# One transformer layer on one core: the next head's loads in sixteen pieces, the softmax division moved to Pool's queue, an output phase with four buffers

## The reference

```python
xn = layernorm(x)                                 # x: 2 x 4096 tokens x 256
q, k, v = (xn @ W.T + b for each of Wq, Wk, Wv)   # 16 heads of 16 channels, q scaled
probs = softmax(einsum('bqhd,bkhd->bhqk', q, k))  # 4096 x 4096 for each of 2 x 16 heads
out = einsum('bhqk,bkhd->bqhd', probs, v)
attn = out @ Wo.T + bo
x = x + attn + routed_ffn(xn)                     # 8 experts, weights from a router
```

## Time and profile before

| | before |
|---|---|
| median of 3 runs | 7455.96 us (7396.34 to 7465.76) |
| the profiled execution | 7403.4 us, its span 7401.6 us |
| PE busy | 6831.7 us, 92% of the span |
| DVE busy | 5743.0 us, 78% |
| ACT busy | 4988.7 us, 67% |
| attention phase | first score about 1511 us, last copy of `pv` at 7058.4 us |
| output phase | 7058.4 to 7401.6 us |

### The profile page before, as it was taken

One profiled execution on the slowest core, in us unless ns is written; L12 is line 12 of the kernel. 1 busy time (PEld: TensorE's weight loads), 2 busy tenths in 40 slices (PEclk: granted clock), 3 DMA queues, 4 the chain that ended last, 5 costly groups with the idle time before them and its releaser, 6 DMA issues. The chain is left out here.

```text
span 7401.6 us, 159847 instructions
## 1 busy us (share of the span) xinstructions
PE 6831.7 (92%) x57168; PEld 3216.6 (43%) x57168; DVE 5743.0 (78%) x6069; ACT 4988.7 (67%) x9109; POOL 423.5 (6%) x367
## 2 busy tenths in 40 slices
PE   7999999699999999999999999999999999999932
PEld 6888888433333333333333333333333333333322
DVE  4544555499989899988898999989889899889611
ACT  3333333168878788877787888878778788778810
POOL 2222322100000000000000000000000000000001
PEclk9999999789989999998898999999889899899965
DMA  2111111111212211111111111122111111111023
GB/s 84 46 46 48 43 41 49 27 21 22 28 21 29 29 22 22 22 22 22 23 22 22 22 22 22 24 31 29 22 22 23 22 22 22 22 22 23 3 88 100
DMA packets 243392, 232.05 MB, mean 31 GB/s; under 512 B 154512, under 2 KB 206992, under 8 KB 236432
## 3 DMA queue, kind: packets, MB, share of 16 engines
q1 hardware_dynamic: 242576, 221.09, 17.9%
HBM read 150.74 MB, written 68.16 MB: 30 GB/s over the span
## 5 line engine op out<-in xcount | busy, mean ns | idle before, releaser
L810 DVE TENSOR_REDUCE mx<-sc 128x1 f32<-128x1024 f32 x4096 | 5007.9, 1224 | 565.8 <-PE sc L699 537.6
L793 ACT ACTIVATE pr<-st 128x512 f32<-128x512 f32 x8192 | 4448.3, 595 | 1046.4 <-PE st L708 763.4
L721 PE MATMUL pv<-pr,vst 128*32 128x256 f32 x32768 | 2761.6, 410 | 14.7 <-ACT oT L780 13.3
L708 PE MATMUL st<-qr,kr 50*128 50x512 f32 x8192 | 2143.9, 518 | 98.8 <-issue 77.4
L699 PE MATMUL sc<-kr,qr 48*128 48x512 f32 x8192 | 1731.4, 417 | 135.2 <-issue 67.9
L708 PEld LDWEIGHTS st<-qr,kr 50*128 50x128 f32 x8192 | 795.3, 190 | 1908.0 <-ACT pr L793 1799.9
L721 PEld LDWEIGHTS pv<-pr,vst 128*32 128x32 f32 x32768 | 661.3, 110 | 1667.1 <-issue 996.1
L699 PEld LDWEIGHTS sc<-kr,qr 48*128 48x128 f32 x8192 | 831.6, 200 | 107.7 <-DVE mx L810 67.3
L393 ACT ACTIVATE gated<-gate 128x512 f32<-128x512 f32 x256 | 152.0, 598 | 637.2 <-PE up L72 637.0
L561 DVE TENSOR_TENSOR hraw<-gated,up 128x512 f32<-128x512 f32 x256 | 173.4, 686 | 431.8 <-ACT gated L393 428.9
L72 PE MATMUL gate<-xT,experts 128*128 128x512 f32 x1536 | 410.5, 404 | 11.3 <-issue 11.3
(11 more groups left out here) (93 smaller groups left out, 1370.2 us busy)
## 6 DMA issues: line engine op xcount, KB each, us to landing
qr<-parts_d SPq DMA_DIRECT2D x192, 256.0 KB, 8.7
kr<-parts_d SPq DMA_DIRECT2D x192, 256.0 KB, 19.5
parts_d<-part SPq DMA_DIRECT2D x64, 512.0 KB, 3.0
x_in<-in_L_attn_hidden_states SPq DMA_DIRECT2D x16, 512.0 KB, 4.5
v_d<-v_sb SPq DMA_DIRECT2D x32, 256.0 KB, 2.1
base_d<-base SPq DMA_DIRECT2D x16, 512.0 KB, 3.2
vst<-v_d SPq DMA_DIRECT2D x32, 256.0 KB, 25.3
sums_d<-oT SPq DMA_DIRECT2D x256, 32.0 KB
```

The source lines that it names most:

```text
L708: nc.tensor.matmul(st[(x + grp) % STB][:, :], kr[par][r0:r0 + ROWSM, kb * P:(kb + 1) * P], qr[par][r0:r0 + ROWSM, q0:q0 + GT], start=True, ...
L721: last = nc.tensor.matmul(pv[VC * j:VC * (j + 1), cols], vst[par][:, kb, :], pr[:, (QSUB * kb + j) % PRING, cols], start=(kb == 0 and half ...
L793: nc.scalar.activation(pr[:, (QSUB * kb + j) % PRING, :], st[x % STB][:, :], ACT.Exp).then_inc(st_read, 1)
L810: nc.vector.reduce_max(mx[par][:, u // MAXU, u % MAXU:u % MAXU + 1], sc[u % 2][:, :], AX.X).then_inc(sc_read, 1)
```

## The change

Attention phase: the twelve loads of q and k are spread over key blocks 1 to 17 of the head's first step, one or two blocks apart, in reversed order, each behind a wait on the count of finished blocks. v is loaded in four parts behind blocks 5, 10, 15 and 20 of the head's second step. The division moves here: for every head Pool's queue loads the 4096 denominators as 128 x 32, DVE inverts them in block 14 of the next head's first step, Pool's queue stores them, loads sums and broadcast reciprocals as 128 x 512 each, POOL multiplies, and the quotients go to a new DRAM tensor `attn_d`. Output phase: two loads for each group instead of nineteen, four buffers instead of two, no loop, results stored from Pool's queue, and PE waits for the sum of group g-2 instead of g-1.

```diff
         QK_LOADS = 2 * 3 * 2
+        V_LOADS = 4
+        QK_EVERY, V_EVERY = 3, 5
...
+            def load(n, par, piece):
+                w, rest = divmod(QK_LOADS - 1 - piece, QK_LOADS // 2)
+                grp, term = divmod(rest, 3)
+                dst, hl = ((qr, (0, 1, 0)), (kr, (0, 0, 1)))[w]
+                r0 = 64 * grp + HD * term
+                sp.dma_start(dst[par][r0:r0 + HD, :].bitcast(F32), c.parts_d[w, hl[term], bass.ds(n * HD, HD), :]).then_inc(qk_loaded, DMA)
+            def load_v(n, par, piece):
+                kbs = KB // V_LOADS
+                sp.dma_start(vst[par][:, piece * kbs:(piece + 1) * kbs, 0:HD],
+                             c.v_d[bass.ds((n // H) * S + piece * kbs * P, kbs * P), bass.ds((n % H) * HD, HD)].rearrange("(t p) d -> p t d", p=P)
+                             ).then_inc(v_loaded, DMA)
...
                     if hf == 0 and not ending:
                         wait_alone(sp, st_full, s * SLOTS + 1, passed)
-                        load(n + 1, 1 - par)
                         wait_alone(sp, pv_done, s * KB + PV_PRE, passed)
-                        load_v(n + 1, 1 - par)
+                        for piece in range(QK_LOADS):
+                            wait_alone(sp, pv_done, s * KB + PV_PRE + 1 + QK_EVERY * piece // 2, passed)
+                            load(n + 1, 1 - par, piece)
                     if not (ending and hf):
                         wait_alone(sp, st_read, s * SLOTS + ROWS_SLOT + 2 + READ_PRE, passed)
                         rows(par if hf == 0 else 1 - par, 1 - hf)
                     sums(s, n, hf)
+                    if hf == 0 and not ending:
+                        for piece in range(V_LOADS):
+                            wait_alone(sp, pv_done, (s + 1) * KB + PV_PRE + V_EVERY * (piece + 1), passed)
+                            load_v(n + 1, 1 - par, piece)
...
+            def divide(n):
+                wait_alone(pool, sums_stored, ((n + 1) * 2 * SUM_STORES + 1) * DMA, passed)
+                nc.gpsimd.dma_start(den[:, :], c.den_d[bass.ds(n, 1), :].rearrange("o (p f) -> (o p) f", p=P)).then_inc(den_in, DMA)
+                wait_alone(pool, den_inverted, n + 1, passed)
+                nc.gpsimd.dma_start(c.rden_d[bass.ds(n, 1), :].rearrange("o (p f) -> (o p) f", p=P), rden[:, :]).then_inc(rden_stored, DMA)
+                nc.gpsimd.dma_start(whole[:, :], c.sums_d[bass.ds(n * HD, HD), :].rearrange("r (x t) -> r x t", t=GT)).then_inc(parts_in, DMA)
+                wait_alone(pool, rden_stored, (n + 1) * DMA, passed)
+                nc.gpsimd.dma_start(recs[:, :], c.rden_d[bass.ds(n, 1), :].rearrange("o (x t) -> o x t", t=GT).broadcast_to([HD, S // GT, GT])).then_inc(parts_in, DMA)
+                wait_alone(pool, parts_in, (n + 1) * 2 * DMA, passed)
+                nc.gpsimd.tensor_tensor(whole[:, :], whole[:, :], recs[:, :], ALU.mult).then_inc(divided, 1)
+                wait_alone(pool, divided, n + 1, passed)
+                nc.gpsimd.dma_start(c.attn_d[bass.ds(n * HD, HD), :].rearrange("r (x t) -> r x t", t=GT), whole[:, :]).then_inc(attn_stored, DMA)
+                wait_alone(pool, attn_stored, (n + 1) * DMA, passed)
+            with pool.Fori(0, HEADS) as n:
+                divide(n)
...
-                                    pe.wait_ge(v_loaded, (n + 1) * DMA)
+                                    pe.wait_ge(v_loaded, (n + 1) * V_LOADS * DMA)
...
+            def inverted(n):
+                dve.wait_ge(den_in, (n + 1) * DMA)
+                if not isinstance(n, int) or n:
+                    dve.wait_ge(rden_stored, n * DMA)
+                nc.vector.reciprocal(rden[:, :], den[:, :]).then_inc(den_inverted, 1)
...
+                        if kb == DIVIDE_AT and q % 2 == 0 and not (first and q == 0):
+                            inverted(RING * i + q // 2 - 1)
 
             rolled(dve, body)
+            inverted(HEADS - 1)
...
+        DEEP = 4
...
+            for g in range(NG):
+                i, b, c0 = g % DEEP, g // GPB, (g % GPB) * GT
+                if g >= DEEP:
+                    sp.wait_ge(low_ready, (g - DEEP + 1) * KC)
+                sp.dma_start(attn[i][:, :, :], c.attn_d[b * D:(b + 1) * D, c0:c0 + GT].rearrange("(k p) t -> p k t", p=P)).then_inc(attn_in[i], DMA)
+                if g >= DEEP:
+                    sp.wait_ge(stored[i], (g // DEEP) * DMA)
+                sp.dma_start(base[i][:, :, :], tokens_of(c.base_d, g)).then_inc(base_in[i], DMA)
+            for i in range(DEEP):
+                sp.wait_ge(stored[i], (NG // DEEP) * DMA)
...
+                pool.wait_ge(sum_ready, g + 1)
+                nc.gpsimd.dma_start(tokens_of(a["out"], g), base[g % DEEP][:, :, :]).then_inc(stored[g % DEEP], DMA)
...
+                pe.wait_ge(low_ready, (g + 1) * KC)
+                if g >= 2:
+                    pe.wait_ge(sum_ready, g - 1)
```

More of the change, by code:

```diff
@@ L878, in output_phase @@
         sum_ready = sem("sum_ready")
-        SUM_LOADS = KC + H
         block = ctx.enter_context(nc.Block())
         def tokens_of(dram, g):
[L883 to L892, removed]
+            return dram[g * GT:(g + 1) * GT, :].rearrange("(t p) d -> p t d", p=P)
@@ L894, in _ @@
         @block.sync
         def _(sp):
[L896 to L916, removed]
@@ L936, in _ @@
-            rolled(pool, body)
+            for g in range(NG):
+                pool.wait_ge(sum_ready, g + 1)
+                nc.gpsimd.dma_start(tokens_of(a["out"], g), base[g % DEEP][:, :, :]).then_inc(stored[g % DEEP], DMA)
         @block.tensor
         def _(pe):
-            def body(g, par, first, last):
-                pe.wait_ge(low_ready, g * KC + KC)
-                pe.wait_ge(sum_ready, g + 1)
+            for g in range(NG):
+                pe.wait_ge(low_ready, (g + 1) * KC)
+                if g >= 2:
+                    pe.wait_ge(sum_ready, g - 1)
@@ L943, in body @@
                 for t in range(TPG):
[L944 to L948 removed]
+                    last = product(nc, ob[g % 2][t // 2][:, t % 2, :], [[v[:, k, t * P:(t + 1) * P] for v in attT[g % 2]] for k in range(KC)],
+                                   [[v[:, k, :] for v in c.woT] for k in range(KC)])
@@ L950, in _ @@
+                last.then_inc(ob_full, 1)
         @block.scalar
         def _(act):
-            def body(g, par, first, last):
-                act.wait_ge(attn_ready, g + 1)
-                if not first:
+            for g in range(NG):
+                act.wait_ge(attn_in[g % DEEP], (g // DEEP + 1) * DMA)
+                if g >= 2:
                     act.wait_ge(ob_full, g - 1)
                 for k in range(KC):
-                    nc.scalar.activation(attT[par][0][:, k, :], attn[par][:, k, :], ACT.Identity).then_inc(high_ready, 1)
@@ L959, in _, with low @@
-            rolled(act, body)
+                    nc.scalar.activation(attT[g % 2][0][:, k, :], attn[g % DEEP][:, k, :], ACT.Identity).then_inc(high_ready, 1)
         @block.vector
         def _(dve):
-            def low(g, par, first):
-                if not first:
+            def low(g):
+                if g >= 2:
                     dve.wait_ge(ob_full, g - 1)
@@ L967, in low @@
                     dve.wait_ge(high_ready, g * KC + k + 1)
-                    nc.vector.tensor_tensor(attT[par][1][:, k, :], attn[par][:, k, :], attT[par][0][:, k, :],
+                    nc.vector.tensor_tensor(attT[g % 2][1][:, k, :], attn[g % DEEP][:, k, :], attT[g % 2][0][:, k, :],
                                             ALU.subtract).then_inc(low_ready, 1)
-            def body(g, par, first, last):
-                if not last:
-                    low(g + 1, 1 - par, first and par == 0)
+            low(0)
+            for g in range(NG):
+                if g + 1 < NG:
+                    low(g + 1)
                 dve.wait_ge(ob_full, g + 1)
-                dve.wait_ge(base_in[par], (g // 2 + 1) * DMA)
+                dve.wait_ge(base_in[g % DEEP], (g // DEEP + 1) * DMA)
                 for i in range(2):
-                    ins = nc.vector.tensor_tensor(base[par][:, 2 * i:2 * i + 2, :], ob[par][i][:, :, :], base[par][:, 2 * i:2 * i + 2, :], ALU.add)
+                    ins = nc.vector.tensor_tensor(base[g % DEEP][:, 2 * i:2 * i + 2, :], ob[g % 2][i][:, :, :],
+                                                  base[g % DEEP][:, 2 * i:2 * i + 2, :], ALU.add)
                 ins.then_inc(sum_ready, 1)
-            dve.sem_inc(sum_ready, 2)
-            for b in range(B):
-                dve.wait_ge(den_in, B * DMA)
-                nc.vector.reciprocal(rden[b][:, :], den[b][:, :]).then_inc(den_inverted, 1)
-            low(0, 0, True)
-            rolled(dve, body)
 class Kept:
```

57 lines of the change are left out of this document (20 added, 37 removed).

## The result

| | before | with the change |
|---|---|---|
| median of 4 runs | 7458.19 us (7396.34 to 7465.76) | 6854.34 us (6827.91 to 6869.44) |
| profiled execution | 7403.4 us | 6869.44 us, span 6867.9 us |
| attention phase, from step 1 to the last copy of `pv` | 5449.8 us | 5163.8 us |
| output phase | 343.2 us | 102.9 us |

The ratio to before is 0.9203, 95% interval 0.9145 to 0.9261. The forecast was 6855 us, range 6790 to 7010.

The account below looks back on a forecast made before the run. Taken as bounds: DVE's maxima per attention step, with code-fetch stalls and low clock at loads, and a chained output phase. 7403.4 - 345 + 8 - 226 = 6840, plus 13, rounded up to 6855 us; range 6790 to 7010.

Parts of the forecast that it names:

- Stalls at loads go: Attention phase, first steps: spreading the loads keeps PE's code packets from waiting behind a burst; gain 345 us, bounds 255 to 368.
- PE's store: Code PE holds in reserve: a burst's delay just exceeds it, judged by head 1's 81.0 us against a looped 84.3 us.
- The rival of the milder stall: Attention first steps: each 256 KB piece still holds a code packet back, 84.3 us a step, 7004 us in all; chance 0.15.
- the one that density does not matter: Rival: PE's "issue" comes with any load, so only the output phase gains, 7198 us; chance 0.05.
- What the jumps leave over: First steps behind the loop's jump back: low clock carried over still costs 3 us each, 40 us in all.
- Reciprocal: DVE in the attention phase: 32 more instructions at 0.25 us with waits, +8 us (5 to 16).
- Output phase: After attention: 16 overlapped groups at 5.4 us, phase 117 us instead of 343, gain 226 us.
- the DMA term 5.2: Output phase: 1.57 MB a group takes 5.2 us of all DMA engines, scaled from 6.9 us for 2.1 MB.
- the 0.8 that I gave as a sign: Output phase: its DMA share would be above 0.8, with the phase at about 117 us.
- From execution to median: Whole kernel: the median was 52.6 us above the profiled execution; a quarter of that, 13 us, was added.
- Pool's stores: Output phase: by a skill page, stores from Pool's queue could wait on DVE, at most its 2.5 us of a group.
- Code: PE's instruction fetch: the skill page's "mostly hidden" was weighed for the rival that stalls are not from load density, chance 0.05.

Follow-up runs that it names:

- pieces alone: Kernel before with only its loads of q, k and v issued in sixteen pieces, everything else as before; 7086.13 us, ratio 0.9544.
- slow burst: Changed kernel plus twelve loads of 16 rows x 16 KB into an unread spare tile in second steps of heads 0 to 30; 7140.6 us.
- fast burst: Changed kernel plus twelve 256 KB loads, each 128 rows x 2 KB, into an unread spare tile in second steps of heads 0 to 30; 6848.33 us.
- bursts of six: Changed kernel with the twelve pieces of q and k issued as two groups of six, at blocks 1 and 10; 6946.3 us.
- burst kept: Changed kernel with the loads of q, k and v again issued all at once in block 0; 7174.07 us, ratio 0.9645.
- two buffers: Changed kernel with two instead of four buffers in the output phase (`DEEP = 2`); 6876.5 us, ratio 0.9245.

## Why the prediction was right

The mechanism held where it was tried, with one correction: not any burst stalls PE, but a slow one. The sum was 29 us too hopeful. The loads were put 58 us too high; the output phase, put 14 too low, the reciprocals, which cost nothing, and the scatter of step 0 made up for half of that.

- *Stalls at loads go.* Right, and shown: plain first steps are at 79.5 us, with pieces alone as well. That the cause is a code packet behind a backlog is shown as far as a trace can: a stall with a slow burst, none with a fast one, and in the gaps followed up no instruction packet for 17 to 27 us until the one that ended the gap. The rival of the milder stall is out, as is the one that density does not matter. Two readings were loose. The 145.3 us of "issue" hold the 13 jumps, 35.3 us; the bursts' share is 110. And head 1's burst without a stall was taken for the measure of PE's store, but it lies outside the loop, where bursts left no gap.
- *What the jumps leave over.* Here a term was mis-sized. I gave the first steps behind a jump 3 us each, 40 in all; they have 1132.0 - 13 x 79.5 = 98 us. So the loads brought 287.2 us and not 345. Before the change the two costs lay partly over each other. In heads 4 and 20 the clock was still 0.50 from the jump while the burst ran (4975 to 5005 us in head 20), and no gap came although code packets lay about 30 us apart: at half the clock the code lasts longer. In the other heads behind a jump the gaps were 2.1 to 4.6 us long, elsewhere up to 5.9. So my comparison of 93.5 with 92.2 us could not show what a jump costs. The amount is also not fixed: in the kernels with pieces and 13 jumps these steps sum to between 1082 and 1132 us, and my 40 us is at the low end of that.
- *Reciprocal.* 0.34 us each, and no cost, where I put 8 us.
- *Output phase.* 102.9 us where I put 117. In its middle 345 GB/s make 16 x 1.57 MB in 73 us, 4.6 a group instead of my 5.4; the DMA term 5.2 was scaled from a phase with many small transfers. Over the whole phase the DMA share is 0.74, not above the 0.8 that I gave as a sign. The first matmul came 28.33 us after the last of the attention phase (I had 25.6), with 5.6 and 3.1 us to landing for Pool's small transfers.
- *Step 0.* Ends 7.4 us earlier; I had left it out, and it is within the scatter told above.
- *From execution to median.* I added 13 us. The median lies 15 below the profiled execution. That and the 29 us by which the sum was too hopeful (563 against 533.7) make 6855 against 6854: the last digits are luck.
- *Pool's stores.* No sign of a delay: they land in 6.1 us beside loads of 6.3 and 7.2 in a queue that is full. The rule of the Trainium skill that I weighed ("SBUF — State Buffer", "A bandwidth-pool intuition that's wrong") did not come to bear.
- *Code.* The Trainium skill, "Runtime: NRT & Kernel Launch", "Instruction fetch mechanics", calls the fetch mostly hidden. The trace agrees in plain steps, which have no gap, and not behind a backlog: 110 of the 145.3 us of waits came from that.

## What to carry to other kernels

When the engine that sets the pace stands still with no semaphore behind it, look at what the DMA queues did in the 10 to 20 us before, and when the last instruction packet came: a prefetch of the next tile that nobody waits for can stop it through its code. Issue such loads a piece at a time, tied to the consumer's progress, and judge them by how long they fill the queue, not by their bytes. Compare steps of equal work by length and granted clock; and when two stalls follow one another, expect that removing one uncovers what the other costs.

## What the runs showed of the hardware

- The same 256 KB land in 14.0 us (median in a burst of twelve) as 16 rows x 16 KB of on-chip memory, and in 4.5 us as 128 rows x 2 KB; from DRAM to DRAM rows of 16 KB went at 262 to 311 GB/s and landed in 4.3 us.
- When PE had run out of code, it started again 2.8 to 3.6 us after the start of the packet that it lacked, in all twelve gaps followed up.
- A short stall of PE can be enough for the granted clock to fall. With bursts of six, in time and then as stretches:

```profile
2010.95 0.39 PE L741 MATMUL sc<-kr,qr 48*128 48x512 f32 x1 [1.53 <-issue]
```

```profile
2012.00:2050.00 38.00, 38.00 (x212) 12.42 (x216) 21.85 (x20) 19.07 (x36) 3.46 (x5) 0.50 0.40 63
```

  1.53 us idle, then 0.50 for 38 us in which PE is busy all the time and DVE still gets only 20 maxima, where a plain step has 30. Other stalls of this size left the clock alone, and after the jumps the low clock lasted a few us in some heads and over 30 in others (changed kernel, heads 8 and 4).
- A plain step takes 79.4 us in some of these kernels and 80.1 in others whose attention phase is the same for PE (the fast burst, the burst kept, two buffers), DVE being busy for 78.4 in all. What sets this was not tried and stays open.
